# Attention outputs normalised twice on VectorE, their low parts on GpSimd

## The reference

```python
q = concat(rope(c_q @ w_qr), c_q @ w_uq)          # c_q = x @ w_dq
k = concat(rope(x @ w_kr), c_kv @ w_uk)           # c_kv = x @ w_dkv
attn = softmax(q k^T * scale)
x = layernorm(x + (attn @ (c_kv @ w_uv)) @ w_o)
g = silu(x @ w1q.T) * (x @ w3q.T)
out = layernorm(x + g @ w2q.T)
```

## Time and profile before

| | us |
|---|---|
| median of 3 runs | 1012.82 |
| lowest, highest | 1012.37, 1015.94 |
| the profiled execution | 1015.77 |
| its span, first to last instruction | 1014.1 |
| PE busy | 923.6 |
| DVE busy | 669.1 |
| ACT busy | 683.2 |
| POOL busy | 651.2 |

### The profile page before, as it was taken

One profiled execution on the slowest core, in us unless ns is written; L12 is line 12 of the kernel. 1 busy time (PEld: TensorE's weight loads), 2 busy tenths in 40 slices (PEclk: granted clock), 3 DMA queues, 4 the chain that ended last, 5 costly groups with the idle time before them and its releaser, 6 DMA issues.

```text
span 1014.1 us, 17542 instructions
## 1 busy us (share of the span) xinstructions
PE 923.6 (91%) x5110; PEld 644.6 (64%) x5110; DVE 669.1 (66%) x1008; ACT 683.2 (67%) x1140; POOL 651.2 (64%) x503
## 2 busy tenths in 40 slices
PE   6989899999999999978989989999999999996985
PEld 3548666666666666657776856665666666665874
DVE  2646677777777777744457577777777777773345
ACT  4536888888888888841333698888888878882132
POOL 0007688888878888750341778888788887863034
PEclk9789999999999999998999999999999999997998
DMA  9653898877877777897000589988777878789001
GB/s 251 186 211 88 157 159 154 147 148 140 155 145 149 145 151 145 151 196 284 23 24 23 132 161 157 151 143 153 143 149 144 153 142 154 140 156 245 11 0 42
DMA packets 419814, 142.24 MB, mean 140 GB/s; under 512 B 405596, under 2 KB 413616, under 8 KB 418736
## 3 DMA queue, kind: packets, MB, share of 16 engines
q1 hardware_dynamic: 418160, 131.11, 65.8%
q10 hardware_dynamic: 1024, 8.39, 2.1%
q0 software_dynamic: 576, 2.10, 0.6%
HBM read 24.38 MB, written 8.13 MB: 32 GB/s over the span
## 4 chain that ended last, share of the span: by engine, by line
PE 62%; issue 13%; DVE 7%; ACT 7%; POOL 3%; DMA 3%; SPq 3%; ACTq 1%; POOLq 0%; DVEq 0%
PE Sb L1065 15%; PE Sa L1065 15%; PE Oa L1094 14%; DVE nmax L776 4%; ACT probs_a L554 3%; PE Ta L1076 2%; PE Sb L1118 2%; PE Sa L1118 2%; ACT P_parts L453 2%; PE Tb L1076 2%; SPq L310 1%; POOL g_lo L429 1%; PE Sb L1194 1%; DMA xr<-in_L_attn_x_dram 1%; DMA w2n<-in_L_ffn_w_dram 1%
## 5 line engine op out<-in xcount | busy, mean ns | idle before, releaser
L387 POOL TENSOR_TENSOR P_parts<-probs_a,P_parts 128x768 f16<-128x768 f32 x128 | 211.9, 1656 | 69.2 <-ACT P_parts L453 69.0
L387 POOL TENSOR_TENSOR P_parts<-probs_b,P_parts 128x768 f16<-128x768 f32 x128 | 211.5, 1654 | 40.0 <-ACT P_parts L453 39.6
L776 DVE TENSOR_REDUCE nmax<-Sb 128x1 f32<-128x1024 f32 x128 | 156.4, 1222 | 56.2 <-PE Sb L1065 56.0
L776 DVE TENSOR_REDUCE nmax<-Sa 128x1 f32<-128x1024 f32 x128 | 155.2, 1212 | 45.5 <-PE Sa L1065 45.3
L1094 PE MATMUL Oa<-PT_dma,V_hi 128*64 128x512 f16 x768 | 132.3, 385 | 0.0
L1065 PE MATMUL Sb<-K_hi,Q_hi 128*128 128x512 f32 x256 | 92.1, 441 | 33.8 <-ACT probs_a L554 30.0
L361 POOL TENSOR_TENSOR turned<-qmul 128x1024 f32<-128x1024 f32 x16 | 38.2, 2410 | 110.0 <-DVE qmul L771 110.0
L453 ACT ACTIVATE P_parts<-probs_a 128x768 f16<-128x768 f32 x128 | 107.4, 839 | 0.0
L453 ACT ACTIVATE P_parts<-probs_b 128x768 f16<-128x768 f32 x128 | 107.2, 840 | 0.0
L554 ACT ACTIVATE probs_a<-Sa,nmax 128x1024 f32<-128x1024 f32 x64 | 71.4, 1115 | 45.7 <-DVE nmax L779 45.6
L554 ACT ACTIVATE probs_b<-Sa,nmax 128x1024 f32<-128x1024 f32 x64 | 71.3, 1115 | 39.8 <-DVE nmax L779 39.5
(11 more groups left out here) (294 smaller groups left out, 1935.6 us busy)
## 6 DMA issues: line engine op xcount, KB each, us to landing
QO<-turned SPq DMA_DIRECT2D x64, 128.0 KB, 2.3
TT<-ternary SPq DMA_DIRECT2D x2, 2304.0 KB, 10.6
PT_dma<-P_parts SPq DMA_TRANSPOSE x256, 3.7
ternary<-tern ACTq DMA_DIRECT2D x1, 2304.0 KB, 8.3
wo<-in_L_attn_w_o_dram SPq DMA_DIRECT2D x4, 512.0 KB, 8.5
xq<-in_L_attn_x_dram SPq DMA_DIRECT2D x2, 1024.0 KB, 9.7
wq_high<-Wq_hi ACTq DMA_DIRECT2D x1, 2048.0 KB, 14.8
Wvo_lo<-wvo_low ACTq DMA_DIRECT2D x2, 1024.0 KB, 7.9
```

The lines of the kernel that those rows point to most:

```text
L387: nc.gpsimd.tensor_tensor(P_parts[:, n % DEEP, 1, :], probs[n % DEEP][:, KP * P:S], P_parts[:, n % DEEP, 0, :], ALU.subtract).then_inc(par ...
L776: nc.vector.tensor_reduce(nmax[:, n % 4:n % 4 + 1], SS[n % 2][:, :], AX.X, ALU.max, negate=True).then_inc(row_max, 1)
```

## The change

`high_out` on GpSimd goes. `normalise` on VectorE runs its `scalar_tensor_tensor` twice on the same Oa: first into O_parts, rounded (this signals `out_hi`), then into QO in fp32 (this signals `out_ready`). `low_out` moves from VectorE to GpSimd, to the places where `high_out` stood (n = 2 and 10, and the two at the end of a batch), and waits there for `out_hi` and `out_ready`. VectorE has no `low_out` any more, neither in the loops nor behind the wait for xr. The splits of the queries stay on GpSimd as they were.

```diff
@@ gpsimd
-                def high_out(group, pair_row, h, last):
+                def low_out(group, pair_row, h):
 
                     cols = slice(h * HALF, (h + 1) * HALF)
+                    hold(pool, out_hi, group + 1)
                     hold(pool, out_ready, OUT0 + group + 1)
-                    if last:
-                        nc.gpsimd.tensor_scalar(O_parts[:, pair_row, cols], QO[:, pair_row + 1, cols], 1.0, 1.0,
-                                                ALU.mult, ALU.mult).then_inc(out_hi, 1)
-                    else:
-                        nc.gpsimd.tensor_copy(O_parts[:, pair_row, cols], QO[:, pair_row + 1, cols]).then_inc(out_hi, 1)
+                    nc.gpsimd.tensor_tensor(O_parts[:, pair_row + 1, cols], QO[:, pair_row + 1, cols],
+                                            O_parts[:, pair_row, cols].bitcast(F), ALU.subtract).then_inc(out_lo, 1)
...
                         if n % 8 == 2 and not first:
-                            high_out(pair * 2 + h - 2, p * 2 - 2, h, False)
+                            low_out(pair * 2 + h - 2, p * 2 - 2, h)
...
                 for h in range(2):
-                    high_out(b * PAIRS * 2 + 2 * PAIRS - 2 + h, 2 * PAIRS - 2, h, True)
+                    low_out(b * PAIRS * 2 + 2 * PAIRS - 2 + h, 2 * PAIRS - 2, h)
                     power(h, b * 4 + h + 1)
@@ vector
-                def low_out(group, pair_row, h):
-
-                    cols = slice(h * HALF, (h + 1) * HALF)
-                    dve.wait_ge(out_hi, group + 1)
-                    nc.vector.tensor_tensor(O_parts[:, pair_row + 1, cols], QO[:, pair_row + 1, cols],
-                                            O_parts[:, pair_row, cols].bitcast(F), ALU.subtract).then_inc(out_lo, 1)
-
...
                     dve.wait_ge(pv_done, PV0 + group + 1)
                     dve.wait_ge(row_ready, ROW0 + group + 1)
+                    nc.vector.scalar_tensor_tensor(O_parts[:, pair_row, h * HALF:(h + 1) * HALF], Oa[:, :], vscale[:, 3:4],
+                                                   rden_row[:, :], ALU.mult, ALU.mult).then_inc(out_hi, 1)
                     nc.vector.scalar_tensor_tensor(QO[:, pair_row + 1, h * HALF:(h + 1) * HALF], Oa[:, :], vscale[:, 3:4],
                                                    rden_row[:, :], ALU.mult, ALU.mult).then_inc(out_ready, 1)
...
                             transposed_low(pair * (TILES // 2) + n // 2, n)
-                        if n % 8 == 6 and not first:
-                            low_out(pair * 2 + h - 2, p * 2 - 2, h)
...
                 dve.wait_ge(xr_in, b * 16 + 16)
-                low_out(group - 2, 2 * PAIRS - 2, 0)
                 attention_rows(0)
                 first_norm(0)
                 normalise(group - 1, 2 * PAIRS - 2, 1)
-                low_out(group - 1, 2 * PAIRS - 2, 1)
```

## The result

The changed kernel takes 985.0 us (median) against 1012.7: a ratio of 0.971, 95% interval 0.968 to 0.974. On a second chip it was 985.3 against 1013.0, ratio 0.972 (0.970 to 0.974). The ratios are worked out from the executions of the faster of two states and are not the quotients of the medians; one of the four of the changed kernel, 996.65 us, was in the slower state. The profiled execution took 981.67, with a span of 980.0.

What follows compares the result with a forecast made beforehand. The prediction took TensorE, busy 91% of the span, as the bound. Loops 8.9, first end 7.5 and second end 6.8 us sum to 23.2, taking the median 1012.82 to 990 us; the 8-in-10 range was 981 to 1002.

Steps and rivals of the forecast that it cites:

- (a): Loops: with low_out off VectorE the next maximum and exponential come earlier; TensorE gains 1.03 us a half.
- (b): Loops, VectorE between PT_lo and the maximum: second normalisation takes 0.66 us, slack 0.05, so TensorE loses 0.61 us.
- (c) to (e): Loops: net 0.42 us a half, x24 = 10.1; pair 1's halves lose 1.2; last pair counted as nothing; together 8.9 us.
- GpSimd's cover: Loops: the subtraction's extra 0.68 us a half on GpSimd is hidden by its 108.6 us of waits for ScalarE's P_parts.
- First end: End of first batch: TensorE's 7.29 us wait for low_out behind xr goes, x1a then decides; 7.5 us gained.
- Second end: End of second batch: the 4.23 us wait goes and the clock's fall with it; 6.8 us gained.
- The loops give nothing: Rival: chain from PT_lo to the maximum grows 0.4 us more, only the ends gain; 999 us, chance 0.14.
- the ends give nothing: Rival: at the batch ends xr lands later or another transfer ends last; 1004 us, chance 0.06.
- the slower one: Rival: the rounding normalisation takes 2.02 us instead of 0.66 beside GpSimd, 28 times, 38 us; 1028 us, chance 0.05.
- The second normalisation is hidden: Rival: all gaps of the loops go, 24.7 us gained there instead of 8.9; 974 us, chance 0.08.
- GpSimd is no cover: Rival: GpSimd's longer work in the loops costs 19 us; 1009 us, no change, chance 0.05.

Runs made afterwards that it cites:

- ends_only: The kernel before with one line moved: VectorE runs the last pair's first low_out ahead of the wait for xr; loops untouched. 1001.6 us, ratio 0.987.
- loops_only: The changed kernel, but GpSimd waits for xr before the low_out of the last pair's first half. 1002.3 us, ratio 0.988 to the kernel before.
- pool_both: The changed kernel without the second normalisation; GpSimd copies the high part, then subtracts. 976.1 us, ratio 0.962 to the kernel before.
- pool_both_again: The same kernel as pool_both, run beside the changed kernel on one chip. 972.3 us, ratio 0.960, against 985.3 for the changed kernel there.
- pool_twice: The changed kernel with a further GpSimd subtraction of 192 columns into a scratch tile ahead of each low_out. 990.3 us, ratio 0.978 to the kernel before.
- third_stt: The changed kernel with a third normalisation on VectorE, of 192 columns into a tile nobody reads. 993.4 us, ratio 0.977 to the kernel before.
- low_out_n4: ends_only with low_out still on VectorE but two tiles earlier, at n = 4 and 12 instead of 6 and 14. 985.8 us, ratio 0.972.

## Why the prediction was right

The range (981 to 1002) holds 985.0, and the mechanisms were those of the forecast: ends_only and loops_only show the two parts of the gain, pool_both the price of the second normalisation. The forecast of 990 was 5 us high. By stage it was 2.0 us short in the loops, 1.5 us too far at the first end and 3.0 short at the second; that the ends nearly cancel is luck.

- **(a) low_out off VectorE.** Right: the gap of 1.00 to 1.04 us is gone at all 24 places, and so is one of 0.57 and 0.55 us in the last pair of each batch, which I had counted as nothing.
- **(b) the second normalisation.** Its size was right (0.67 us apart at 310.82 and 311.49, 746 ns), its cost not: 0.61 was forecast and 0.51 is what pool_both gives, so the slack was 0.15 and not 0.05. I read the slack off one half, and only at its last link. TensorE is already held a little one step earlier: pool_both_again, with a single normalisation, has 1.89 us from its Sa to its Sb scores just before the normalisation (305.46 to 307.35), the changed kernel 1.73 at the same place (309.49 to 311.22). A gap that the new work swallows is slack too. The lines, pool_both_again and then after:

```profile
305.46 0.73 PE L1053 MATMUL Sa<-K_hi,Q_hi 128*128 128x512 f32 x2
...
307.35 0.72 PE L1053 MATMUL Sb<-K_hi,Q_hi 128*128 128x512 f32 x2
```

```profile
309.49 0.73 PE L1054 MATMUL Sa<-K_hi,Q_hi 128*128 128x512 f32 x2
...
311.22 0.74 PE L1054 MATMUL Sb<-K_hi,Q_hi 128*128 128x512 f32 x2
```

- **(c) to (e), sum of the loops.** 8.9 forecast, 10.9 measured. A half in the loops went from 21.36 to 20.87 us, which is 0.49 instead of 0.42, and 24 x 0.07 = 1.7 is most of the difference.
- **GpSimd's cover.** Right for the attention stage, by pool_both and pool_twice. The subtraction was put at 1294 ns and took 1274.
- **First end.** 7.5 forecast, 6.0 measured. The wait for L795 went, but the wait for Wvo_lo before it, which I had taken as fixed, was 3.61 instead of 1.7 us, and the granted clock was at half for some 3 us behind it. So TensorE and not x1a came last (no wait at 455.96). The row of after:

```profile
441.00:442.00 1.00, 1.00 (x7) 0.50 1.14 213
```

- **Second end.** 6.8 forecast, 9.8 measured. The fall of the clock at 934 is gone as forecast; besides, the wait for Wvo_lo was 2.66 instead of 3.96 us and the clock was up again (0.84) in the stretch from 903 after a restart at 900.4, where before it was only on its way (0.66) in the stretch from 930 after a restart at 924.6. The rows after, against the earlier trace rows:

```profile
899.00:900.00 1.00, 0.00 (x0) 0.96 1.40 34
900.00:901.00 1.00, 0.58 (x2) 0.50 1.19 218
...
903.00:904.00 1.00, 1.00 (x9) 0.84 1.14 210
```

 Both ends together, 15.7, are near the 14.3 that were forecast: what I called fixed moved up at one and down at the other.
- **The rest.** 1.6 us came from stages that I had not costed. Most of it is in the last one, which runs from 62.5 to 64.8 us over the traces and is at 62.5 in ends_only too, where `low_out` is still on VectorE; it can't be put down to the change.
- **Rivals.** "The loops give nothing", "the ends give nothing" and the slower one are out by the stages. "The second normalisation is hidden" is out by third_stt and pool_both. "GpSimd is no cover", to which the rule of the Trainium skill would lead (page "GPSIMD Engine Reference", section 4.1 Engine selection), fell: the rule has the duration right (1274 against 0.69 us), and pool_both, which gives GpSimd still more, is the fastest kernel here.

## What to carry to other kernels

Read from the gap of the bound engine back to the instruction that is late, and price the change on that chain; the same instruction may cost nothing a few places on or on an engine that waits anyway. Before a step is moved to another engine, try another place for it on its own engine, and try giving all of it to the engine that has room: here the first, with the wait for xr moved, equalled the change, and the second beat it by 13 us. An instruction that stands behind a wait it does not need can cost far more than its siblings in the loops (here 6.0 and 9.8 us at the two ends, about 1.0 us at each of the 24 places), so look at the unrolled ends of a loop by themselves.

## What the runs showed of the hardware

L795's duration in the kernel before is no property of its own: it ends about 0.55 us after the GpSimd instruction that runs when it starts. This holds for all 28 that start beside one; the four that start beside none take 0.69 us. The timeline of before, three starts of L795 that the rows ahead of the prediction do not have, or not with their neighbour:

```profile
316.38 1.65 POOL L387 TENSOR_TENSOR P_parts<-probs_b,P_parts 128x768 f16<-128x768 f32 x1
```

```profile
422.67 1.66 POOL L387 TENSOR_TENSOR P_parts<-probs_b,P_parts 128x768 f16<-128x768 f32 x1 [0.66 <-ACT P_parts L453]
423.21 1.66 DVE L795 TENSOR_TENSOR O_parts<-QO,O_parts 128x512 fp32r<-128x512 f32 x1
...
441.25 1.64 POOL L387 TENSOR_TENSOR P_parts<-probs_a,P_parts 128x768 f16<-128x768 f32 x1 [0.84 <-ACT P_parts L453]
442.20 1.24 DVE L795 TENSOR_TENSOR O_parts<-QO,O_parts 128x512 fp32r<-128x512 f32 x1
```

GpSimd ends at 318.03, 424.33 and 442.89; L795 ends at 318.57 (316.52 + 2.05), 424.87 and 443.44, that is 0.54, 0.54 and 0.55 us later. The GpSimd instruction that already runs is not longer for it (1.64 to 1.66 us). VectorE waits here until the other instruction has ended, and doesn't merely run slower beside it. The Trainium skill, page "SBUF — State Buffer", section Who interferes with whom, calls the shared ports an exclusive lock, and the trace agrees. The normalisations, with one input in SBUF, stay at 740 to 753 ns.

It works the other way too. In low_out_n4 a GpSimd copy of the queries (L353) starts 0.60 us before L795 ends, and takes 1.07 us; where L795 doesn't overlap it, it takes 0.60 to 0.62. This happens 24 times there. The timeline of low_out_n4, beside L795 from 326.40 to 328.26:

```profile
326.06 1.66 POOL L387 TENSOR_TENSOR P_parts<-probs_a,P_parts 128x768 f16<-128x768 f32 x1 [1.13 <-ACT P_parts L453]
327.66 1.07 POOL L353 CAST Q_hi<-QO 128x512 fp32r x1
```

The same code at the start of the kernel took 70.6 to 79.0 us. The mean granted clock of the stage was 0.87 in before (76.8 us) and 0.98 in after (70.8 us), but 0.91 in the longest, so the clock alone doesn't explain the spread, and its cause stays open. A difference of one pair of traces is therefore read by stage and not from the spans.
